# Weights split and edges searched in the first stage, and the source logits of 67 edge columns gathered by GpSimd in the projection

## The reference, cut to what matters

```python
xn = layernorm(x)                                   # 3125 x 1024
xp = (xn @ W).reshape(N, 4, 256)
a_src, a_dst = einsum('nhc,hc->nh', xp, att_src), einsum('nhc,hc->nh', xp, att_dst)
e = leaky_relu(a_src[src] + a_dst[dst], 0.2)        # edges and self loops
m = segment_max(e, dst); ee = exp(e - m[dst]); z = segment_sum(ee, dst)
out = segment_sum(xp[src] * (ee / z[dst])[:, :, None], dst) + bias
x = x + relu(out)
x = x + mx_quantise(layernorm(x)) @ mx_quantise(weight).T + bias
```

## Time and profile before

| | |
|---|---|
| median of 3 runs | 1378.39 us (1376.91 to 1381.05) |
| the profiled execution | 1382.31 us, span 1380.6 us |
| mean granted TensorE clock | 0.982 |
| busy over the span | PE 1286.5 us, PEld 901.2, DVE 1089.6, ACT 1005.5, POOL 679.2 |
| first stage | from 0 to 133.86 us of the span |
| projection | from 133.86 to about 485 us |

### The profile page before, as it was taken

The page is one execution under the profiler, slowest core; times in us unless marked ns, Lnnn a source line. Parts: engine busy times, 40 slices in busy tenths (PEclk is TensorE's granted clock), DMA queues, the critical chain, the costliest instruction groups (busy, mean ns, idle before and its releaser), DMA issues. The chain is left out here.

```text
span 1380.6 us, 29656 instructions
## 1 busy us (share of the span) xinstructions
PE 1286.5 (93%) x10194; PEld 901.2 (65%) x10194; DVE 1089.6 (79%) x2255; ACT 1005.5 (73%) x2253; POOL 679.2 (49%) x610
## 2 busy tenths in 40 slices
PE   7898888889999969999999899999998699999997
PEld 5776444544444458888888788888887244444553
DVE  6998899889883478888888788888886977777771
ACT  3566987886455568889998789988996566666662
POOL 1000731111227477777777777777774344444441
PEclk9899999999999989999999999999999899999999
DMA  7686586443355579999999999999999477777743
GB/s 256 227 298 197 148 311 223 159 159 116 132 208 190 227 252 383 388 360 376 366 380 369 384 396 383 367 362 342 385 359 383 152 184 189 192 186 190 191 111 53
DMA packets 110549, 363.62 MB, mean 263 GB/s; under 512 B 20204, under 2 KB 20988, under 8 KB 110148
## 3 DMA queue, kind: packets, MB, share of 16 engines
q0 software_dynamic: 66048, 225.15, 46.9%
q1 hardware_dynamic: 40996, 135.71, 28.7%
q10 hardware_dynamic: 3360, 0.91, 0.2%
HBM read 299.78 MB, written 72.85 MB: 270 GB/s over the span
## 5 line engine op out<-in xcount | busy, mean ns | idle before, releaser
L1786 PE MATMUL sum_ps<-xg,wgt 128*128 128x256 f16 x4992 | 560.4, 273 | 16.3 <-DMA xg<-d_xp,tables 9.2
L1757 ACT ACTIVATE wgt<-hot,tables 128x128 f16<-128x128 f16 x1664 | 502.2, 388 | 73.5 <-DVE hot L1701 64.6
L1786 PEld LDWEIGHTS sum_ps<-xg,wgt 128*128 128x128 f16 x4992 | 472.3, 98 | 72.5 <-DMA xg<-d_xp,tables 9.8
L1682 POOL DMA_INDIRECT xg<-d_xp,tables x404 | 417.4, 1033 | 128.2 <-issue 121.7
L1555 PE MATMUL xp_ps<-acc 128*128 128x512 f16 x1152 | 265.9, 382 | 8.3 <-DVE acc L1110 4.1
L1741 DVE TENSOR_TENSOR acc<-sum_ps,acc 128x1024 f32 x220 | 268.8, 1222 | 1.8 <-issue 1.6
L2184 PE MATMUL fmm_ps<-xg,tables 128*128 128x512 f16 x1200 | 263.1, 379 | 1.4 <-DVE tables L2013 1.4
L2184 PEld LDWEIGHTS fmm_ps<-xg,tables 128*128 128x128 f16 x1200 | 117.3, 98 | 137.9 <-issue 1.9
L1555 PEld LDWEIGHTS xp_ps<-acc 128*128 128x128 f16 x1152 | 108.5, 98 | 126.3 <-DVE acc L1145 5.1
L1712 DVE TENSOR_TENSOR wgt<-hot,tables 128x512 f16<-128x512 f16 x416 | 157.5, 417 | 0.0
L1740 DVE TENSOR_TENSOR zsum<-z_ps,zsum 128x8 f32 x220 | 36.2, 165 | 98.6 <-PE z_ps L1796 97.5
(11 more groups left out here) (326 smaller groups left out, 1602.3 us busy)
## 6 DMA issues: line engine op xcount, KB each, us to landing
d_xnT<-acc SPq DMA_DIRECT2D x25, 512.0 KB, 3.7
tables<-d_lo SPq DMA_DIRECT2D x40, 320.0 KB, 4.2
own_row<-d_own SPq DMA_DIRECT2D x25, 512.0 KB, 5.3
wdT<-in_x_dram SPq DMA_DIRECT2D x24, 512.0 KB, 5.1
acc<-d_xnT SPq DMA_DIRECT2D x24, 512.0 KB, 5.3
d_xp<-acc SPq DMA_DIRECT2D x24, 512.0 KB, 2.8
d_own<-acc SPq DMA_DIRECT2D x24, 512.0 KB, 4.3
xr<-in_x_dram SPq DMA_DIRECT2D x24, 512.0 KB, 6.6
```

Source lines behind the costliest of these rows:

```text
L1682: nc.gpsimd.indirect_dma_start(out=xg[s][u][:, :, :].rearrange("p a n -> p (a n)"), out_offset=None, in_=d_xp, in_offset=bass.IndirectOffs ...
L1757: last = nc.scalar.activation(wgt[k % WB][:, u, h, :], hot[k % TURN][:, u, :], ACT.Copy, scale=col(numT[:, h, :], u, q))
L1786: last = nc.tensor.matmul(sum_ps[s][:, h * C:(h + 1) * C], w[:, u, a * HEADS + h, :], x[u][:, b, h * C:(h + 1) * C], start=(u == 0 and h % ...
```

## The change

In the first stage the one-hot counting is gone. Instead, `dst` is seen as 250 lines of 200 edges. SP loads the last edge of each line (two DMAs of 125 numbers, `line_i`), DVE compares them with all node numbers (`passed`, two operations of 125x3200), PE counts the lines that lie wholly at or below each node (`count_lines`, 50 matmuls with one column each, in turn 0), DVE turns the count into a line number in turn 2 (`lines_of`), POOL gathers that line for each node (25 indirect DMAs of 128 rows of 800 bytes, three buffers), and DVE counts in it with one comparing operation for each tile (`count_line`, 128x200 with an accumulated output, 25 in the turns 6 to 23). POOL also makes more constants first (node numbers 128x3200 among them), ahead of the zeros that it stores in `d_head`.

Into the turns go: `w_top` on ACT in the turns 5, 7, ..., 19, and `w_rest` on DVE in the turns 6, 8, ..., 20; the powers in the turns 1 and 3, the source digits in turn 4, the plan's start in turn 5; the turning of the low digits in turn 10, on PE and in turn 11 on ACT. The store to `d_lo` is ahead of the last five stores. The loops of DVE and ACT are written out.

In the projection there are 65 units in place of 79: 4 in tile 0, 6 in each of the tiles 1 to 10, 1 in tile 11. The other 67 edge columns are gathered by POOL, one indirect DMA of 128 rows of 32 bytes each (`sources`): 19 ahead of the first `divide`, and 16 after each of the first three `multiply`s, ahead of the next `divide`. `spread_heads` waits for all of them (`side_in`).

```diff
-HCOLS = 17
-HBATCH = 24
+LINE = 200
+LINES = 125
+SETS = E // (LINE * LINES)
 UCOLS = 5
-UNITS = -(-EC // UCOLS)
+UNITS = 65
+SIDE = UNITS * UCOLS
+SIDE_COLS = EC - SIDE
...
+    FIRST_W = 5
+    LOWS_AT = 10
+    parted = {FIRST_W + 2 * c: c for c in range(KC)}
...
+            pool.wait_ge(line_ready, 1)
+            for t in range(TILES):
+                if t >= SEGS:
+                    pool.wait_ge(tallied, t - SEGS + 1)
+                nc.gpsimd.indirect_dma_start(
+                    out=seg[t % SEGS][:, :], out_offset=None, in_=dst.rearrange("(r c) -> r c", c=LINE),
+                    in_offset=bass.IndirectOffsetOnAxis(ap=line_at[:, t:t + 1], axis=0)).then_inc(seg_in[t % SEGS], 16)
...
-            def one_hot(b, s):
-                dve.wait_ge(lo_free, b + 1)
-                hots(hot_lo[s][:, :, :], dlo[:, bass.ds(b * HCOLS, HCOLS), :], HCOLS, P).then_inc(lo_ready, 1)
+            def lines_of():
+                dve.wait_ge(made, 4)
+                dve.wait_ge(plan_summed, 1)
+                own.link(nc.vector.tensor_scalar(line_of[:, :], hist_ps[:, 4 * KC:4 * KC + TILES], float(SETS * LINES - 1), None, ALU.min))
+                nc.vector.tensor_copy(line_at[:, :], line_of[:, :]).then_inc(line_ready, 1)
+
+            def count_line(t):
+                dve.wait_ge(seg_in[t % SEGS], 16 * (t // SEGS + 1))
+                if t >= 1:
+                    dve.wait_ge(tallied, t)
+                nc.vector.tensor_scalar(below[:, :], seg[t % SEGS][:, :], node_id[:, t:t + 1], 0.0, ALU.is_le, ALU.add,
+                                        accum_out=tally[:, t:t + 1]).then_inc(tallied, 1)
+
+            counted = lambda t: min(TILES, max(0, -(-(t - 5) * TILES // (TILES - 1 - 6))))
...
-                one_hot(t, s)
+                if t == 2:
+                    lines_of()
+                for k in range(counted(t - 1), counted(t)):
+                    count_line(k)
...
+            for t in range(TILES - 1):
+                turn(t)
+                if t == 1:
+                    weight_powers()
+                if t == 3:
+                    row_powers()
+                if t == 4:
+                    source_digits()
+                if t == 5:
+                    plan_start()
+                if t - 1 in parted:
+                    w_rest(parted[t - 1])
...
+            for t in range(TILES - 1):
+                turn(t, t % XS, 16 * ((t - 3) // 2 + 1) if t >= 3 else None, first=t if t < XS else None)
+                if t == FIRST_W:
+                    act.wait_ge(w_powers, 1)
+                if t in parted:
+                    w_top(parted[t])
+                if t == LOWS_AT + 1:
+                    turn_lows()
...
+            def count_lines():
+                pe.wait_ge(passed_ready, 1)
+                for t in range(TILES):
+                    for k in range(SETS):
+                        last = nc.tensor.matmul(
+                            hist_ps[:, 4 * KC + t:4 * KC + t + 1], passed[0:LINES, k, t * P:(t + 1) * P], ones_b[0:LINES, :],
+                            start=(t == 0 and k == 0), stop=(t == TILES - 1 and k == SETS - 1), skip_group_check=True)
+                last.then_inc(plan_summed, 1)
...
-    FIRST_UNITS, NEXT_UNITS, BUSY = 4, 7, 11
+    FIRST_UNITS, NEXT_UNITS, PLACES, BUSY = 4, 6, 7, 11
+    SIDE_AHEAD, SIDE_TURN = 19, 16
...
+            def sources(columns):
+                for c in columns:
+                    gather(side[:, c, :], d_node, src1[:, SIDE + c:SIDE + c + 1], side_in)
+
+            sources(range(0, SIDE_AHEAD))
             divide(0)
             for t in sorted(quant):
...
                 multiply(o)
+                at = SIDE_AHEAD + SIDE_TURN * o
+                sources(range(min(SIDE_COLS, at), min(SIDE_COLS, at + SIDE_TURN)))
                 if o + 1 < KC:
                     divide(o + 1)
...
             def spread_heads():
-                nc.vector.tensor_scalar(edge, edge, table_inverse[:, :], None, ALU.mult)
+                dve.wait_ge(side_in, 16 * SIDE_COLS)
+                nc.vector.tensor_scalar(asrc[:, 0:SIDE, :], asrc[:, 0:SIDE, :], table_inverse[:, :], None, ALU.mult)
+                nc.vector.tensor_copy(asrc[:, SIDE:EC, :], side[:, :, 0:HEADS])
```

More of the change, by code:

```diff
@@ L555, in turn @@
                                                op0=ALU.mult, op1=ALU.mult).then_inc(rstd_ready, 1)
-                one_hot(t, s)
-            with dve.Fori(0, TURNS - 1) as i:
-                back = own.enter(i, XS * (STAT_LINKS + ROOT_LINKS))
-                for j in range(XS):
-                    turn(i, j)
-            own.leave(back, TURNS - 1)
-            for j in range(XS):
-                turn(TURNS - 1, j, last=True)
-            root(TILES - 1, 0)
-            dve.wait_ge(most_spread, 1)
@@ L687, in turn, with w_top, turn_lows @@
                     keep(t - 2, j % 2)
-            for t in range(XS):
-                turn(t, t, 16 if t == 3 else None, first=t)
-            with act.Fori(1, TURNS) as i:
-                for j in range(XS):
-                    turn(XS * i + j, j, 16 * (2 * i + (j - 1) // 2))
+            def w_top(c):
+                nc.scalar.activation(w16[:, c, 0, :], w[:, c, :], ACT.Copy, scale=w_scale[:, :]).then_inc(w_high, 1)
+            def turn_lows():
+                act.wait_ge(src_lo_turned, 1)
+                nc.scalar.activation(lo_turned[:, :], hist_ps[:, 0:LO_ROWS], ACT.Copy).then_inc(src_lo_kept, 1)
+            for t in range(TILES - 1):
[6 more added lines that the diff above has]
+                    turn_lows()
             norm(TILES - 1, 0)
@@ L926, in project @@
         first_in = sem("first_in")
+        side_in = sem("side_in")
         ends_in = sem("ends_in")
@@ L1316, in _ @@
             prepare(1)
-            w_rest(1)
-            for c in range(KC):
-                if c + 2 < KC:
-                    w_rest(c + 2)
-                if c == KC - 1:
+            for n, u in enumerate(units(0)):
+                if n == 1:
                     x_rest(1)
-                if c % 2:
-                    unit(units(0)[c // 2])
+                unit(u)
             for t in range(1, BUSY + 1):
                 todo = list(units(t))
-                for s in range(NEXT_UNITS):
+                for s in range(PLACES):
                     if s < len(todo):
@@ L1404, in _ @@
         def _(act):
-            def w_top(c):
-                nc.scalar.activation(w16[:, c, 0, :], w[:, c, :], ACT.Copy, scale=w_scale[:, :]).then_inc(w_high, 1)
             def x_top(t):
```

257 lines of the change are left out of this document (130 added, 127 removed).

## The result

| | before | changed |
|---|---|---|
| median of the runs | 1378.83 us (1376.91 to 1381.05) | 1361.86 us (1361.67 to 1366.51) |
| ratio, 95% interval | | 0.9877 (0.9862 to 0.9892) |
| the profiled execution | 1382.31 us, span 1380.6 | 1366.51 us, span 1364.7 |

What follows compares the result with a forecast made beforehand. DVE was taken to lead in both stages, with other engines near. First stage +3.2 and projection -20.0 gave -16.8 us: 1365.5 from the profiled 1382.3, or 1361.6 in terms of the runs' median; range 1355 to 1368.

Steps and rivals of the forecast that it cites:

- before the turns: Ahead of turn 0: two comparisons replace `hot_hi`, and the zero store is put off from W's loads: -0.8 us.
- turns 0 to 5: First stage: DVE's `lines_of` waits for `count_lines` on PE, and moved work joins the turns; turn 6 starts later: +3.2 us.
- row: Turns 6 to 20: `w_top` on ACT and `w_rest` on DVE wait in sequence, 6.97 us a pair against 6.92: +0.4.
- counts: Turns 6 to 20: DVE's `count_line`s, taken at 0.45 us each, lie mostly under the wait for `w_top`: +0.6 us.
- loads of x: Turns 6 to 20: gathered lines add DMA time, x lands later with no room to spare: +2.5 us.
- turn 21 to the second stage: End of first stage: PE's shorter turns without split and one-hots, -1.7 us; earlier `d_lo` store no longer holds the barrier, -1.0.
- tiles 1 to 10, units: Projection: one unit fewer a tile saves DVE 1.68 us, less 1.5 in all for PE and ACT close behind: -15.3 us.
- GpSimd's first divide: Projection: 19 gathers ahead make GpSimd's divide 4.3 us late, so ACT waits in `grid_w`, in tile 5 alone: +3.5 us.
- 1: First stage: late x loads or dear count operations set the turns, +12 us in place of +3.2, 1370.4 total; chance 0.12.
- 2: Projection: POOL becomes the bound from 1.52 us a gather on; at 2.0 us each, 1395 us total; chance 0.06.
- 3: Projection: units don't set a tile, PE and ACT take over: -8 us in place of -15.3, 1368.9 total; chance 0.14.
- 4: First-stage turns: PE's clock falls to 1.2 GHz as its work shrinks: +30 us, 1392 total; chance 0.02.

Runs made afterwards that it cites:

- units_only: The kernel before with only the projection's part: 65 units and 67 columns gathered by GpSimd; first stage and W split in tile 0 stay. 1361.16 us, ratio 0.9846.
- six_x_tiles: The changed kernel with six buffers for x in place of four. 1364.24 us, ratio 0.9886.
- best_lines_later: Changed kernel plus six x buffers, 12 gathers before first divide, `d_head` load after it, line-end loads after W's second chunk, third before edges. 1358.74 us, 0.9844.
- head_behind_divide: The changed kernel with GpSimd's load of `d_head` moved behind the first divide, from ahead of the 19 side gathers. 1362.50 us, ratio 0.9855.
- units78: The changed kernel with 78 units in place of 65 and 2 side gathers in place of 67; first stage stays. 1378.4 us, ratio 0.9988.
- lines_twice: The changed kernel with each gather of 128 lines of `dst` issued twice, the second copy unread but waited for. 1367.10 us, ratio 0.9909.

## Why the prediction was right, term by term

The changed kernel's profiled execution against that of before; negative is faster.

| term | predicted | measured |
|---|---|---|
| before the turns | -0.8 | +0.8 |
| turns 0 to 5 | +3.2 | -0.1 |
| turns 6 to 20: row +0.4, counts +0.6, loads of x +2.5 | +3.5 | +3.8 |
| turn 21 to the second stage | -1.7 - 1.0 | -3.2 |
| tile 0 | -3.3 | -3.7 |
| tiles 1 to 10, units | -15.3 | -13.8 (units_only) |
| GpSimd's first divide | +3.5 | 0; +1.4 in tile 4 |
| tiles 11 to 14 | -4.9 | -5.1 |
| sum | -16.8 | -19.9; -17.0 by medians |

The two sums, -16.8 and -17.0, are closer than their terms, and that part is luck. By the profiles the terms add up to -19.9: turns 0 to 5 and GpSimd's divide came out 5.4 us better than forecast, the start and the units 3.1 worse, the other terms 0.8 better. The 2.9 us from there to the medians are the open point at the end.

**The turns.** The direction held: there was no gain from relieving DVE. That turns 6 to 20 came out at +3.8 for my +3.5 is luck too. The loads of x are about 2 of it (six_x_tiles), near my 2.5. The row of `w_top` and `w_rest` with its counts, which I had at +1.0, came out at -0.6: a pair takes 6.77 us and not 6.97. What filled the gap is the turning of the low digits, about 2.4 us in six_x_tiles by the rows of turns 13 and 14. It stood in my description of the change and had no term in the sum; that PE turns the digits behind a tile's logits while ACT stands for them, I hadn't seen. Turns 0 to 5 were mis-sized. PE's `count_lines` took 1.40 us, not 1.7 to 2.5, and tile 0's logits ended at 45.15, not 45.7:

```profile
42.47 2.68 PE L825 MATMUL lg_ps<-acc,wa 128*8 128x128 f32 x16
45.08 1.40 PE L833 MATMUL hist_ps<-ones_b,acc 125*128 125x1 bf16 x50
46.60 0.18 DVE L556 TENSOR_SCALAR line_of<-hist_ps 128x25 f32<-128x25 f32 x1 [2.91 <-PE hist_ps L833]
46.91 0.69 DVE L574 BATCH_NORM_STATS2 stats<-wdT 128x6 f32<-128x512 f32 x1
```

Turn 3 starts at 46.91, where I had 48.6, and turn 6 at 57.41, where I had 59.9. The wait is there, 2.9 us long, with the root of tile 3 behind it; it is only shorter. **Before the turns** I had the sign wrong. I saw what goes (the zero store and one-hots) and missed what comes: two loads of 125 single values each ahead of the second chunk of W. best_lines_later shows that they hold it up; how much of the later start is theirs, one execution doesn't settle.

**The projection.** One unit fewer a tile is worth 13.8 us in ten tiles when nothing else is late (units_only), 1.5 less than my term. GpSimd's first divide was the term that failed here. My sum had GpSimd free at 218.2 us in the times of the kernel before, 84.3 us into the stage, and missed by ACT from 213.9 on, 80.0 into it. A gather cost what I said, and when GpSimd is that late the wait does come (4.0 us at 85.1, six_x_tiles). But in the changed kernel it was free at 80.6: the gathers began 55.6 us into the stage, where the kernel before had GpSimd free at 58.7, and took 25.0 us in place of 25.65. And DVE had the divide's input ready only at 80.9. The late digits of tile 4 have a part in that: without them it is 78.9, and ACT waits 1.2 us (head_behind_divide, where tile 0 was 0.8 us shorter too). The digits are loaded by SP's queue behind 1 MB of weights, 1 MB of stores and a tile of x, while GpSimd's `d_head` fills the same DMA engines. I hadn't counted that queue's backlog, although the kernel before shows a wait of ACT at the same place (195 to 225 us):

```profile
ACT oh L1456 <- DMA tables<-d_lo: 1.4, 1, 1.4
```

Of the signs that I had named, the pairs took 7.5 us in the mean and not 7.0, turn 6 started at 57.4 and not near 60, ACT didn't wait for GpSimd in tile 5, and the second stage began at 135.2 and not near 137; tiles 1 to 3 took 14.8 to 15.1 us as forecast, and tile 4 didn't.

**The rivals.** 1: the first stage came out at +1.3 and +2.5 in the two executions, so no. 2: no wait of ACT for GpSimd with 16 gathers; it begins before 22. The neighbours that I named there do hold a gather up, `x_rest` to 2.0 us and a mask to 1.14 (six_x_tiles), but few gathers begin beside them, and the mean stayed at 1.32 us. 3: out by units78. 4: turns 6 to 20 have a mean clock of 0.97, so no, though not untouched: it was at 1.2 GHz for 3.4 us in turns 13 and 14. Lower clocks were seen in lines_twice (0.91) and behind longer waits of PE in the projection.

**What stays open.** By the profiles, 19.8 us are won up to the end of tile 23, by the medians of whole runs 17.0. The profile of before may have had a long first stage: units_only, with the same turns, reached its second stage 1.8 us earlier, though its store of `d_lo` is smaller too. And the rest spreads over 6 us between executions. One profile a kernel can't settle which of the two it is. Why the clock was lower behind some of PE's pauses of 1.9 to 4 us and not behind others wasn't settled either. Nor was the price of the low digits' turning: the kernel with it at another place is the run to make next.

## What to carry over

When you relieve the leading engine, write down for every stretch how far below it the next resource is. Here the loads of x were 0.3 us a turn behind DVE, and what was taken from DVE there won nothing, while in the projection one unit less gave 1.4 us a tile. Give every small operation that you move a term of its own: the digits' turning is half a microsecond of work on PE and on ACT, and made each wait for the other. Put a queue's backlog into the sum when a transfer must land in time: what stood ahead of the digits was eight times their size. And a late engine may be hidden by another delay, as in head_behind_divide; find it before you mend that delay, or the mending will seem worth nothing.
